# SyncE's paddings of experts 0 to 7 in one run, and the order of its register and weight loads behind them, in a two-layer mixture-of-experts kernel

## The reference

```python
x = x + 0.5 * _L0_ffn_ref(_layernorm(x), norm_w, gate_w, gate_b, w1, b1, w2, b2)
x = x + _L0_attn_ref(_layernorm(x), w_q, w_k, w_v, w_o)
x = x + 0.5 * _L0_ffn_ref(_layernorm(x), norm_w, gate_w, gate_b, w1, b1, w2, b2)

def _L0_ffn_ref(x, ...):              # 16 experts, 4 for each token
    t = xf * rsqrt(mean(xf * xf) + EPS) * norm_w
    vals, idx = top_k(t @ gate_w.T + gate_b, 4)
    G = zeros(M, E).at[arange(M)[:, None], idx].set(softmax(vals))
    h = einsum('mh,eoh->emo', t, w1) + b1
    a, b = minimum(h[..., ::2], LIMIT), clip(h[..., 1::2], -LIMIT, LIMIT)
    y = einsum('emi,edi->emd', a * sigmoid(ALPHA * a) * (b + 1.0), w2) + b2
    return x + einsum('me,emd->md', G, y)
```

## Time and profile before

| | us |
|---|---|
| median of 3 runs | 843.39 |
| the three runs | 840.59, 843.39, 849.29 |
| profiled execution | 843.22 |
| its span | 841.5 |
| TensorE busy | 715.8 (85%) |
| VectorE busy | 583.3 (69%) |
| ScalarE busy | 439.8 (52%) |
| GpSimd busy | 402.7 (48%) |

### The profile page before, as it was taken

The page is one execution under the profiler, slowest core; times in us unless marked ns, Lnnn a source line. Parts: engine busy times, 40 slices in busy tenths (PEclk is TensorE's granted clock), DMA queues, the critical chain, the costliest instruction groups (busy, mean ns, idle before and its releaser), DMA issues.

```text
span 841.5 us, 17945 instructions
## 1 busy us (share of the span) xinstructions
PE 715.8 (85%) x4745; PEld 564.9 (67%) x4745; DVE 583.3 (69%) x1375; ACT 439.8 (52%) x1066; POOL 402.7 (48%) x449
## 2 busy tenths in 40 slices
PE   2456538999999999789998898788679999999996
PEld 2444326778778887667776576556458888888883
DVE  3857518877777777457886675574867777777777
ACT  3564405655555555337675554444625555555551
POOL 5765762545455546432345421433644554444452
PEclk9999879999999999999999887888899999999999
DMA  7968947968876462464442332216657787778677
GB/s 308 373 242 323 314 171 249 329 209 317 297 252 223 167 208 88 146 247 152 151 165 94 123 113 96 90 41 218 206 184 232 253 276 258 241 260 246 231 253 255
DMA packets 77917, 181.02 MB, mean 215 GB/s; under 512 B 12016, under 2 KB 36864, under 8 KB 73856
## 3 DMA queue, kind: packets, MB, share of 16 engines
q1 hardware_dynamic: 39904, 96.21, 33.8%
q0 software_dynamic: 14928, 49.97, 15.6%
q10 hardware_dynamic: 22992, 33.70, 12.3%
HBM read 97.60 MB, written 65.45 MB: 194 GB/s over the span
## 4 chain that ended last, share of the span: by engine, by line
PE 44%; DVE 6%; another core or an unknown queue 3%; issue 3%; ACT 1%; DMA 1%; SPq 0%; POOL 0%; DVEq 0%; ACTq 0%
PE s_psT L1242 13%; PE s_psG L1269 6%; PE s_psO L1839 3%; PE s_psS L1804 3%; PE s_psS L1190 2%; PE s_psG L1776 2%; PE s_psS L1204 2%; PE s_psT L1820 2%; DVE s_a_nm L2072 2%; PE s_psT L1824 2%; PE s_psG L1886 1%; PE s_psG L1789 1%; PE s_psR L1911 1%; PE s_psG L1862 1%
## 5 line engine op out<-in xcount | busy, mean ns | idle before, releaser
L1242 PE MATMUL f_bank<-weights,f_e_th 128*128 x316 | 120.1, 477 | 18.4 <-issue 17.1
L1455 POOL DMA_INDIRECT kbuf<-f_e_ys,f_e_place x79 | 79.9, 1011 | 108.4 <-ACT f_e_ys L1405 94.4
L1455 POOL DMA_INDIRECT kbuf<-s_e_own_ys,s_e_own_place x79 | 78.7, 996 | 94.4 <-ACT s_e_own_ys L1405 81.5
L2072 DVE TENSOR_REDUCE s_a_nm<-s_psS 128x4 f32<-128x1024 f32 x64 | 78.3, 1223 | 56.4 <-PE s_psS L1804 42.9
L1242 PE MATMUL s_psT<-s_e_own_weights,s_e_own_th 128*128 x316 | 113.4, 458 | 4.3 <-issue 4.2
L1689 POOL DMA_INDIRECT rows<-s_a_row,s_a_slot_i x64 | 63.7, 995 | 106.5 <-DVE s_a_slot_i L2199 88.2
L1316 DVE TENSOR_TENSOR f_e_hb<-f_bank,f_e_bias 128x512 f32<-128x512 f32 x79 | 54.3, 687 | 57.2 <-PE f_bank L1242 35.1
L1242 PEld LDWEIGHTS f_bank<-weights,f_e_th 128*128 128x128 f32 x316 | 61.9, 197 | 41.1 <-issue 23.5
L2346 ACT ACTIVATE s_a_pT<-s_psT 128x1024 f32<-128x1024 f32 x62 | 63.3, 1021 | 43.4 <-PE s_psT L1824 31.5
L1316 DVE TENSOR_TENSOR s_e_own_hb<-s_psT,s_e_own_bias 128x512 f32<-128x512 f32 x79 | 54.2, 687 | 41.5 <-PE s_psT L1242 40.2
L736 POOL DMA_INDIRECT rows<-f_r_row,f_r_slot_i x64 | 65.9, 1029 | 34.9 <-issue 18.1
(11 more groups left out here) (401 smaller groups left out, 1841.4 us busy)
## 6 DMA issues: line engine op xcount, KB each, us to landing
s_e_own_weights<-w_split SPq DMA_DIRECT2D x12, 1024.0 KB
w_split<-weights ACTq DMA_DIRECT2D x7, 1536.0 KB
s_e_tb<-rows ACTq DMA_DIRECT2D x68, 144.0 KB
f_e_tb<-rows ACTq DMA_DIRECT2D x62, 144.0 KB
s_a_qs<-s_a_qk SPq DMA_DIRECT2D x32, 256.0 KB, 2.6
weights<-w_raw SPq DMA_DIRECT2D x10, 768.0 KB, 14.7
w_split<-weights POOLq DMA_DIRECT2D x5, 1536.0 KB, 8.8
s_a_ks<-s_a_qk SPq DMA_DIRECT2D x30, 256.0 KB, 2.4
```

The lines of the kernel that those rows point to most:

```text
L1242: last = pe.matmul(psH[j][:, :], left[:, p % 2, j, k * P:(k + 1) * P], first_of(h, k)[:, bass.ds(at, 1), :], start=n == 0, stop=n == len(p ...
L1455: pool.indirect_dma_start(out=kbuf[:, :], out_offset=bass.IndirectOffsetOnAxis(ap=place[:, i % KEPT:i % KEPT + 1], axis=0), in_=ys[:, n, : ...
L2072: dve.tensor_reduce(nm[:, b % 2, :, :, j].rearrange("p t o -> p o t"), src, X_AXIS, ALU.max, negate=True).then_inc(s_mx, 1)
```

## The change

`range(FIRST)` is experts 0 to 3, `range(2 * FIRST)` experts 0 to 7 (FIRST is 4). Both places that wrote the first four paddings on SyncE now write eight; the semaphores stay (`pad0` for 0 to 3, `pad1` for 4 to 7). In the expert loop, the call for experts 4 to 7 is gone. At pair 2, SyncE first reads the registers that it read at pair 3 before, then waits for `pad1` and orders pair 2. Expert 11's raw load moves from before pair 2's order to behind it.

```diff
--- before.py
+++ after.py
@@ -578,7 +578,7 @@
         first_biases(sp)
         split.load(sp, 10)
         sp.wait_ge(s_ends, 1)
-        pad_rows(sp, m.phase, table, rows, c, s_pad, some=range(FIRST))
+        pad_rows(sp, m.phase, table, rows, c, s_pad, some=range(2 * FIRST))
 
     @program.add("vector")
     def _(dve):
@@ -1094,13 +1094,11 @@
         first_row(sp)
         for p in range(BY_SP):
             if p == 2:
-                if first_layer:
-                    split.load(sp, 11)
-                pad_rows(sp, f"{m.phase}_more", table, rows, c, routed.s_pad, some=range(FIRST, 2 * FIRST))
-                routed.other_rows(sp, (1,))
-            if p == 3:
                 load_needs(8, min(16, 2 * BY_SP))
                 at.load(1)
+                routed.other_rows(sp, (1,))
+            if p == 3 and first_layer:
+                split.load(sp, 11)
             if p == 4:
                 routed.other_rows(sp, (2,))
             if p == 8:
@@ -1647,7 +1645,7 @@
         sp.wait_ge(s_t, B * HP)
         early_loads(sp)
         sp.wait_ge(routed.s_ends, 1)
-        pad_rows(sp, m.phase, table, rows, c, routed.s_pad, some=range(FIRST))
+        pad_rows(sp, m.phase, table, rows, c, routed.s_pad, some=range(2 * FIRST))
 
     def sum_parts(engine, ch, b):
```

## The result

The change made the kernel slightly slower, not faster. Over 20 runs of each on one chip the kernel before takes 840.10 us (837.43 to 849.29) and the changed one 843.96 us (841.34 to 848.32): a ratio of 1.0042, 95% interval 1.0026 to 1.0057, some 3.5 us. The time lies inside the range and near the value that I gave for "nothing moves", but the direction was wrong.

The account below looks back on a forecast made before the run. An expert loop's opening was taken as bound by waits, its long rest by TensorE. From 843.22 us, 3.0 (first layer) and 0.5 (second layer) were taken off: 839.7 us, range 827 to 850.

Parts of the forecast that it names:

- nothing moves: First-layer slow stretch holds TensorE's next signals until the scatter is over, second layer hangs on ScalarE's copy: 843 us; chance 0.19.
- Its step begins 4.85 us earlier than now: First layer: with pair 2's rows there by 96.3, TensorE begins pair 2's step at 99.3 in place of 104.15.
- I lean to the middle: 3.0 us: First layer: worth of the 4.85 us inside the slow stretch, between 1.4 us and all of it.
- TensorE's start ... moves by 0 to 5.2 us; I take 1.5: First layer: TensorE's start, at 87.99 before, comes later because paddings 4 to 7 precede the first rows.
- Eight paddings: SyncE's queue, first layer: four took 4.10 us, so eight end at 82.4 and first rows are fetched near 85.9, not 84.54.
- the slow stretch: First layer, about 98 to 126 us: TensorE's signals 7 to 12 us late, SyncE crawls, while GpSimd scatters without a break.
- The Trainium skill's rule on rings: Rings consume descriptors in order, so the first rows pay for paddings ahead of them: the 5.2 us end of TensorE's delay.
- Pair 2's rows: First layer: ordered near 89.7 in place of 97.59, there by 96.3; TensorE's 6.33 us wait for them goes.
- theory B: Experiments' rival: the moved loads of expert 11 and registers are to blame; paddings alone like the base or 1 to 2 us faster.
- Expert 11's load: First layer: ordered at about 91 in place of 86.76, cost nothing; if cover is gone, up to 2.7 us on ScalarE.
- Second layer: Four more paddings cost nothing; pair 2's rows go out up to 4 us sooner; gain between 0 and 2.8, taken as 0.5 us.
- The late start decides: Rival, first layer: four extra issues and 576 KB ahead of first rows start TensorE 5.2 us late: 849 us; chance 0.15.

Follow-up runs that it names:

- e2_order_only: On the kernel before with bounded registers: paddings 4 to 7 stay at pair 2, register loads behind them, expert 11's load behind pair 2; 850.41 us, 1.0050.
- e1_pads_only: On the kernel before with bounded registers: only paddings 4 to 7 moved early, both layers; expert 11's load and register loads stay; 851.06 us, 1.0065.
- e5_pads_behind_pair0: The change with bounded registers, but paddings 4 to 7 behind pair 0's order and ahead of pair 1's, both layers; 849.37 us, 1.0047 to the kernel before.
- the base: The kernel before with a bound on each register that a wait compares with (578 register instructions more); 850.06 us, 1.0043 to the kernel before.
- a7_change_sync_tells: The whole change with bounded registers, SyncE itself waiting for first ranks and paddings in place of GpSimd; 793.68 us, 1.0050 to the kernel before.
- e9_tells_pads_behind: Bounded registers, SyncE's own wait in place of GpSimd's, paddings 4 to 7 behind pair 0, expert 11's load behind pair 2; 792.58 us, 1.0029 to kernel before.
- b1_mended_again: The kernel before with bounded registers, run again on the fourth chip; 847.62 us, 1.0042 to the kernel before.
- the seven pauses: The kernel before with bounded registers and seven pauses in GpSimd's last first-layer scatters, run on two chips; 809.09 us, 1.0244, and 810.45 us, 1.0260.
- e11_tells_too: Bounded registers, paddings 4 to 7 behind pair 0, expert 11's load ahead of pair 2, SyncE's own wait in place of GpSimd's; 862.82 us, 1.0209 to kernel before.

## Why the prediction was wrong

**The step that failed** is the one from pair 2's rows to pair 2's step: "Its step begins 4.85 us earlier than now", of which "I lean to the middle: 3.0 us". It began 0.18 us earlier (103.97 against 104.15). I had it wait for the rows and for nothing else. What it waited for, once the rows were there, was TensorE's own signal of pair 1's transposes, 5.2 us late, and ScalarE's copy behind it. With it went a term that was too small: "TensorE's start ... moves by 0 to 5.2 us; I take 1.5" was 3.10 us in the profiled pair and 2.9 in the mean of four traces of each side.

*Eight paddings.* I took them as 8.2 us. They took 9.33 us here and 8.6 to 9.5 in the six other traces that have them, on both kinds of chip, so this is no matter of the slow stretch. Four took anything from 3.1 to 6.2 us. First rows were ordered at 86.80, 0.9 us after my 85.9.

From order to use they took 4.29 us against 3.45 (84.54 to 87.99). The Trainium skill's rule on rings, that each consumes its descriptors in order ("DMA: Bandwidth & Descriptors", "Queues, rings and completion order"), would have added 2.3 us by my reading. No such price shows: in four traces of each opening on the slower chips it was 3.45 to 4.99 us behind four paddings and 3.86 to 4.96 behind eight, on the faster ones 4.7 to 5.1 and 3.5 to 4.1.

*Pair 2's rows.* They were out by 92.35, against my 89.7, and the 6.33 us wait went, as forecast. But I let the slow stretch begin at 98 us, a fixed time, and so had TensorE's signal for pair 1 prompt. In the changed kernel ScalarE reads it 5.2 us late, at 103.03; in the four traces with the changed opening it is 4.1 to 6.8 us late, in the four with the old one 0 to 3.6. It would be natural that SyncE's earlier row orders bring this on, but the parts speak against it: `e2_order_only` orders pair 2's rows at 100.78 and has the signal 7.0 us late, `e1_pads_only` at 90.95 and 2.1 us late. What brings it on stays open. That the early rows gain nothing on such a chip, to within 0.4%, is what `e5_pads_behind_pair0` shows: pair 2's transposes at 100.0, start not late, time equal to the base.

*What costs is the paddings' place* ahead of the first rows: 0.48% plus or minus 0.43 on one chip, 0.46 plus or minus 0.36 on another, against kernels with the paddings behind pair 0. The likely way is the late start. The slow stretch ends about when GpSimd's scatters do (SyncE's last slow instruction is at 119 to 126 us in every trace of these chips), so a kernel that has started 3 us late can have one tile fewer done when it ends. Four traces against four put this at 2.8 us at tile 12 and 1.6 us at the layer's end. But `e1_pads_only`, with the same late start, is not behind at either mark and has no loss clear of noise. That the late start does it without the moved loads of expert 11 and the registers (theory B) is not shown.

*Expert 11's load* was cost at nothing, and ScalarE did not wait for it in the changed kernel, nor in `a7_change_sync_tells`. But the cover is thin: with pair 2 ahead of it ScalarE waited 8.6 us in `e5_pads_behind_pair0` and 3.7 in `e2_order_only` on the slower chips, 3.6 in `e9_tells_pads_behind` on a faster one, all more than my bound of 2.7.

*Second layer.* Four paddings more cost 4.4 us of issue and not 1.9, but what lay between them and the first rows hid most of it: from the first padding to the first transposes it is 13.0 to 13.1 us in four traces with the old order and 13.3 to 13.5 in four with the new. The gain of 0.5 isn't shown. Pair 1's step was 1.0 us earlier in the one trace, but from the first padding to tile 12 the new order takes 47.4 to 51.3 us and the old one 48.1 to 51.1. With that layer alone changed the kernel is at +0.20%, inside the interval.

**What the rivals got right.** "The late start decides" had the sign, and a start of 5.2 us for the 3.1 measured. It put the loss at 5.5 us, where 3.5 were measured. "Nothing moves" said why pair 2's gain vanishes: the slow stretch holds TensorE's signals. The two together fit best, and I had let them stand apart. That the measured 843.96 lies so near the 843 of "nothing moves" is luck: I reckoned from 843.22, and the kernel before takes 840.10 over the longer series.

**What stays open.** The first layer accounts for 1.6 of the 3.5 us. The rest has no row. From tile 78 to the second layer's first transposes the four executions with the old opening take 284.8, 284.7, 283.8 and 285.6 us, those with the new one 283.3, 289.3, 286.7 and 288.7. This length follows the time that the block spends at 1.2 GHz: 54.6 us of it go with 283.3 and 283.8 us, 61.4 with 284.8 to 287.8, and 68.3 with 289.3 twice, once in `e5_pads_behind_pair0`, which has no late start. Nothing shows that a later start causes it. The cause of the slow stretch itself is open too.

## What to carry to other kernels

Before moving work ahead of a critical order, measure how long the issuing engine takes for the longer row of DMAs: in the second layer eight took 6.3 us where four took 1.94. And a wait that ends inside a stretch bound by something else can be worth nothing when it goes; ask what that stretch is bound by, and which signal is the next to be late. Four traces of each side, compared at a mark, told more than the two profiles, and a part tried alone (`e1_pads_only`) can still fail to show what the whole shows.

## What the runs showed of the hardware

Chips differ more than any edit did: the kernel before took 845.6, 845.5 and 845.3 us on three and 789.7 and 789.3 us on two others, with a mean granted clock of 0.944 against 0.980 over its runs. On the slower kind SyncE's register instructions took 0.7 us and TensorE's signals came up to 19 us late while GpSimd scattered without a pause beside other small transfers. How much of this a trace shows varies: in one of the base (`b1_mended_again`) pair 2's copy was prompt, at 106.7 us. None of the six traces on the faster kind shows any of it.

The slow stretch is only a part of what sets the kinds apart. Without the seven pauses tile 12 is at 149 to 155 us on the slower kind (161.6 in `e11_tells_too`) and at 132 to 135 on the faster, some 17 us. From tile 78 to the second layer's first transposes it is 283 to 289 us with 55 to 68 of them at 1.2 GHz, against 251 to 252 us with 14 to 17.

In single traces, the gain that pair 2's rows were to bring showed only on the faster kind. No kernel here beat the kernel before; the nearest on its kind of chip was `e9_tells_pads_behind` at 1.0029, with the added register instructions, whose cost on that kind no run measured.
